# Second cross attention of a two-layer decoder: two steps of the query quantization move from VectorE to GpSimd

## What is computed

```python
def _fq_sym(x, axis):
    s = jnp.max(jnp.abs(x), axis=axis, keepdims=True) / 127.0
    s = jnp.maximum(s, 1e-08)
    q = jnp.clip(jnp.round(x / s), -127.0, 127.0) * s
    return x + jax.lax.stop_gradient(q - x)
...
q = (x @ Wq + bq).reshape(1, B * N, H, hd)      # 2048 rows, 16 heads of 16
kv = (cond @ Wkv + bkv).reshape(1, -1, 2, H, hd)  # 512 keys for all rows
...
attn = jax.nn.softmax(attn.astype(jnp.float32), axis=-1)
attn = _fq_unsigned(attn, axis=-1)
```

## Time and profile before

| | |
|---|---|
| median of 3 runs | 1367.86 us (1361.7 to 1369.36) |
| profiled execution: its own time | 1366.42 us |
| profiled execution: span | 1364.3 us |
| mean granted TensorE clock | 0.916 of full |
| second cross attention, first limit to last exponential | 781.4 to 1109 us |
| busy: TensorE / VectorE / ScalarE / GpSimd | 84% / 66% / 46% / 42% of the span |

### The profile page before, as it was taken

How to read it: one execution, slowest core, us unless ns; L and a number is a source line. 1 busy time by engine, 2 the same in 40 slices (tenths; PEclk the granted TensorE clock), 3 DMA queues, 4 the chain that set the end, 5 groups by cost and what they waited for, 6 DMA issues and landing times.

```text
span 1364.3 us, 24773 instructions
## 1 busy us (share of the span) xinstructions
PE 1140.4 (84%) x7640; PEld 809.8 (59%) x7679; DVE 898.8 (66%) x2501; ACT 632.9 (46%) x1432; POOL 577.2 (42%) x886
## 2 busy tenths in 40 slices
PE   3699989994999999668887677877777778999988
PEld 2577767772566666446665345655555554788755
DVE  5576764774432333388877399999999864656657
ACT  3165654331211111225554498988889851433300
POOL 6143542248211111125565354466655653455500
PEclk8799999995999999879898789888889778999989
DMA  5866735013111111265441300000000014455454
GB/s 146 199 202 157 198 106 175 27 48 110 52 47 47 47 42 44 79 176 152 120 127 33 125 4 1 6 29 33 29 18 29 25 40 136 128 161 157 146 180 144
DMA packets 75805, 127.10 MB, mean 93 GB/s; under 512 B 11703, under 2 KB 59063, under 8 KB 72279
## 3 DMA queue, kind: packets, MB, share of 16 engines
q1 hardware_dynamic: 62142, 95.13, 25.3%
q0 software_dynamic: 10272, 28.39, 5.7%
q10 hardware_dynamic: 3264, 2.01, 0.5%
HBM read 76.97 MB, written 48.13 MB: 92 GB/s over the span
## 4 chain that ended last, share of the span: by engine, by line
PE 56%; issue 12%; ACT 9%; POOL 9%; DVE 6%; DMA 5%; SPq 2%; ACTq 1%; POOLq 0%; DVEq 0%
PE ps L228 17%; PE ps L1173 15%; PE ps L1190 7%; ACT work L1917 6%; POOL work L1951 3%; PE ps L482 3%; POOL xs_scratch L1511 2%; PE ps L1182 2%; PE ps L1158 2%; DMA W<-work 2%; PE ps L495 1%; PE ps L464 1%; DVE work L608 1%; DMA W<-q_parts 1%; PE ps L508 1%
## 5 line engine op out<-in xcount | busy, mean ns | idle before, releaser
L1173 PE MATMUL ps<-W,work 128*128 x628 | 227.5, 495 | 1.6 <-issue 1.4
L1917 ACT ACTIVATE work<-ps,work 128x512 f32<-128x512 f32 x256 | 205.1, 821 | 40.4 <-POOL work L1951 39.1
L1529 POOL DMA_INDIRECT ys_scratch<-work x118 | 113.1, 958 | 260.2 <-DVE work L1373 113.4
L1855 DVE TENSOR_REDUCE work<-ps 128x1 f32<-128x512 f32 x256 | 172.7, 681 | 14.3 <-PE ps L1762 8.1
L1423 DVE TENSOR_TENSOR work<-work,ps 128x128 f32<-128x128 f32 (+1 forms) x118 | 49.7, 421 | 199.2 <-ACT work L1492 198.6
L608 DVE TENSOR_REDUCE work<-ps 128x2 f32<-128x512 f32 (+1 forms) x192 | 127.2, 685 | 71.4 <-PE ps L464 70.2
L787 POOL TENSOR_SCALAR_AFFINE_SELECT work<-work 128x256 f32<-128x256 f32 (+1 forms) x192 | 92.6, 485 | 157.5 <-ACT work L721 156.4
L1951 POOL TENSOR_SCALAR work<-work 128x1 f32<-128x1 f32 x256 | 99.8, 390 | 128.3 <-DVE work L1855 113.0
L1173 PEld LDWEIGHTS ps<-W,work 128*128 128x128 f32 x628 | 110.9, 191 | 68.9 <-issue 63.1
L721 ACT ACTIVATE work<-ps 128x512 f32<-128x512 f32 x192 | 110.6, 599 | 66.6 <-PE ps L482 66.0
L1492 ACT ACTIVATE work<-ps 128x128 f32<-128x128 f32 (+1 forms) x118 | 45.3, 384 | 164.7 <-PE ps L1173 164.7
(11 more groups left out here) (261 smaller groups left out, 2398.9 us busy)
## 6 DMA issues: line engine op xcount, KB each, us to landing
work<-xs_scratch SPq DMA_DIRECT2D x79, 132.0 KB, 2.2
W<-ys_scratch SPq DMA_DIRECT2D x16, 512.0 KB, 3.8
q_parts<-work SPq DMA_DIRECT2D x48, 128.0 KB, 1.9
W<-in_w_in SPq DMA_DIRECT2D x6, 1024.0 KB, 11.2
W<-q_parts SPq DMA_DIRECT2D x15, 384.0 KB
work<-xs_scratch SPq DMA_DIRECT2D x39, 130.0 KB, 2.1
W<-k_parts SPq DMA_DIRECT2D x8, 512.0 KB
W<-in_w_out SPq DMA_DIRECT2D x1, 4096.0 KB, 18.9
```

The costliest lines, as they stand in the source:

```text
L1173: mm = q.e.matmul(PS[bks[c]][:, 0:N], self.XT[s % 2][:, k, :], w[:, k, bass.ds(regs[s] + 512 * c if c else regs[s], N)], start=k == 0, sto ...
L1529: q.e.indirect_dma_start(YS[L], bass.IndirectOffsetOnAxis(ap=self.dst[n % self.NY], axis=0), self.YB[n % self.NY], None).then_inc(*landing ...
L1855: q.e.tensor_reduce(self.mm[:, h:h + 1], PS[banks.of["c1_s", t, h]][:, :], AX, ALU.max, negate=True).then_inc(*up("c1_mx", t, h))
L1917: q.e.activation(self.ee[n // 2 % 3][:, 512 * (h % 2):512 * (h % 2) + 512], PS[banks.of["c1_s", t, h]][:, :], ACT.Exp, bias=self.nb[:, h:h ...
```

## The change

VectorE's `dve_queries` ends with the reciprocal, which now raises the event "c1_rq". The multiplication and the rounding are issued by GpSimd in a new function `pool_queries`: the multiplication in round 8, ahead of a scatter where there is one, the rounding in round 9, and the clamp in round 10 as before, now behind GpSimd's own chain instead of VectorE's event. For tile 0 both are issued ahead of the first clamp. Operands, types and values are the same.

```diff
                 q.wait_ge(at("c1_sq", t))
-                e.reciprocal(self.rq, sq).then_inc(*q.step())
-                yield
-                q.wait_ge(q.chain())
-                e.tensor_tensor(q3, q3, bc(self.rq, 2, 16), ALU.mult).then_inc(*q.step())
-                yield
-                q.wait_ge(q.chain())
-                e.tensor_scalar(qf, qf, MAGIC, MAGIC, ALU.add, ALU.subtract).then_inc(*up("c1_qr", t))
+                e.reciprocal(self.rq, sq).then_inc(*up("c1_rq", t))
...
+            def pool_queries(self, q, t):
+
+                q3 = heads(self.qf, 16)
+                q.wait_ge(at("c1_rq", t))
+                q.e.tensor_tensor(q3, q3, bc(self.rq, 2, 16), ALU.mult).then_inc(*q.step())
+                yield
+                q.wait_ge(q.chain())
+                q.e.tensor_scalar(self.qf, self.qf, MAGIC, MAGIC, ALU.add, ALU.subtract).then_inc(*q.step())
+
             def pool_Q3(self, q, t):
-                q.wait_ge(at("c1_qr", t), at("c1_z"), at("c1_qt", t - 1))
+                q.wait_ge(q.chain(), at("c1_z"), at("c1_qt", t - 1))
...
                 pool_numbers(q, 1)
+                queries = [self.pool_queries(q, 0)]
+                steps(queries, 9)
                 self.pool_Q3(q, 0)
...
+                    if h == 8 and t + 1 < T:
+                        queries = [self.pool_queries(q, t + 1)]
+                    steps(queries)
                     if h == 10 and t + 1 < T:
                         self.pool_Q3(q, t + 1)
```

## The result

The changed kernel takes 1384.62 us (median of 4 runs, 1382.65 to 1389.89) against 1368.61 us of the kernel before (median of 4 runs, 1361.7 to 1375.82). The ratio is 1.0122, with a 95% interval of 1.0063 to 1.0182. Timed once more beside other kernels it was 1.0089 (1.0058 to 1.0119), so the loss is 12 to 17 us. The forecast was 1371, 3 us above before, and the range ended at 1383.

A forecast was written before the change was run, and what follows sets the result against it. VectorE has almost no idle time, but GpSimd, in order inside the head loop, is crowded in rounds 8 to 12. Terms 2.0 + 0.6 + 1.2 - 0.5 + 1.1 = +4.4 us on 1366.4 gave 1371, range 1362 to 1383.

The forecast's parts named there:

- That is where the two instructions are put: GpSimd, inside the head loop, crowded in rounds 8 to 12; TensorE waited 1.91 us for Q3, ScalarE 2.12 for a limit.
- The likeliest case: The forecast of 1371 us together with its neighbour, the start alone at about 1368; chance 0.60, own range 1365 to 1375.
- the second rival: GpSimd's burst in rounds 8 to 10 becomes the bound in full: +10 to +19 us, 1377 to 1386; chance 0.27.
- start: Tile 0, where nothing else runs: GpSimd's two instructions delay Q3 and all rounds by 1.1 us (bounds 1.0 and 1.3).
- tiles 0 to 2: Less LayerNorm and routing around; limit 7 to Q3 needs 3.2 us against 2.45: +0.4 us each, 1.2 in all.
- tile 3: No scatter, and limit 9 waited 1.32 us for VectorE: the cover holds, the whole 0.53 us is won, -0.5.
- even tiles from 4 on: GpSimd needs 3.2 us from limit 7 to Q3 instead of 2.75, limit 7 comes 0.34 earlier: +0.1 each, 0.6.
- odd tiles from 5 on: Five tiles with scatters: Q3 starts 0.16 us later, plus the port, +0.4 each (between +0.16 and +0.76), 2.0 in all.
- the reckoning from limit 7 to Q3: GpSimd's queue of limits, multiplication, rounding and what lies between, ahead of Q3: 3.2 us in even tiles, Q3 +0.16 in odd.
- the next is due two rounds later: VectorE's L1860 is done before GpSimd's rounding, so no term for a blocked L1860; otherwise 15 x 0.55 = 8 us.
- a Q3 held up by L1860: Odd tiles: L1860 comes 0.53 us earlier, ahead of Q3, which may stand behind it for up to 0.6 us.
- VectorE's 8 us turn into idle time: The 8.0 us of room freed on VectorE become idle time ahead of work that GpSimd releases later.

The follow-up runs named there:

- again: The changed kernel, profiled and timed a second time against the kernel before: ratio 1.0089, stage stretch +14.1 us.
- the version with the cheap operation: The changed kernel with GpSimd's rounding replaced by a clamp of the same operands, queries not rounded: 1.0027 of the kernel before, stage +3.4 us.
- the relief: From the changed kernel, GpSimd's multiplication and rounding taken out too, so neither engine does them: 0.9916 of the kernel before, stage -6.1 us.
- both sides: The changed kernel with VectorE also keeping both instructions, into a scratch tile: 1.0135 of the kernel before, stage +19.0 us.
- two rounds earlier: The changed kernel with its three GpSimd instructions in rounds 6, 7 and 8 instead of 8, 9 and 10: 1.0039 of the kernel before, stage +5.3 us.
- the run meant to part them: The changed kernel with TensorE's transposes of Q3 moved from round 12 to 14, ScalarE's copy from 13 to 15: 1.0308 of before, stage +43.2 us.
- the better kernel: The kernel before with only the multiplication on GpSimd and no scatter in rounds 8 and 10: 1362.88 us against 1371.85, ratio 0.9945.
- the one with the moved scatters: The changed kernel with the scatters of rounds 8 and 10 moved to later even rounds: 1.0027 of the kernel before, 1.0031 when run again.

## Why the prediction was wrong

- **Bound and place.** "That is where the two instructions are put" held, and so did VectorE's freed room becoming partly idle time. The likeliest case was forecast at 0.60 and the second rival, GpSimd's burst as the bound, at 0.27 with 1377 to 1386 us. The result is that rival's: (13.1 - 1.1) / 15 = 0.8 us a tile, where it had 0.6 to 1.23.
- **Prices of the instructions.** 0.62 and 1.14 us were forecast, 0.620 and 1.084 measured. The start was +1.1, and it is: from the first L1836 to the first Q3 2.19 us before, 3.32 after.
- **The terms of the sum**, against the growth of the stretches in the two profiles of the change (us; tile 14 ends behind the stage stretch):

| term | forecast | the change | again |
|---|---|---|---|
| start | +1.1 | +1.1 | +1.1 |
| tiles 0 to 2 | +1.2 | +1.1 | +2.7 |
| tile 3 | -0.5 | -0.4 | -0.4 |
| even tiles from 4 on | +0.6 | +4.1 | +3.9 |
| odd tiles from 5 on | +2.0 | +7.2 | +6.9 |

- **The step that failed** is the reckoning from limit 7 to Q3 in the even and odd tiles. Even tiles: 3.2 us forecast, 3.78 measured. Odd tiles: 4.44 forecast (4.28 + 0.16, before the allowance of about 0.25 for ports), 5.35 measured. In both most of the missing time is in instructions that got longer because they now overlap a VectorE rounding: limit 9 by 0.5 us, the power by 0.46, a scatter by 0.28. The text had the rule and the rows for it, and then gave it no term because "the next is due two rounds later". That is true of the GpSimd rounding, which met no VectorE rounding in tiles 6 and 7, and false of limit 9 and the power behind it. The term that it did have, a Q3 held up by L1860, isn't what happened: Q3 takes 0.83 us as before. That tiles 0 to 2 came out right in the first profile is luck: their three stretches grew by 1.08, -1.15 and 1.20.
- **Not seen at all:** the slow pairs in the rounds after the burst, where I had let the loss end at Q3. Of the 1.61 us that odd tile 7 grew by, 1.09 stand at Q3; it was 0.6 us shorter than before once the scatters were moved away and no slow pair was left. The growth of the odd tiles goes with the slow pairs in most of the table (13 slow pairs and 1.6 us a tile with the change, 1 and 0.1 us with the rounding alone), but that they are all of it isn't shown: the version with the cheap operation has 13 too, and its odd stretches grew by only 0.65 us.
- **"VectorE's 8 us turn into idle time"** was wrong in the other direction. Alone the relief is worth 6.1 us of stage and 0.84% of the time, and against "both sides" the change still gets 5.9 us of stage for it. By the forecast's own terms the GpSimd work was priced at 4.4 + 8.0 = 12.4 us; it costs 19.0, that is (19.0 - 1.1) / 15 = 1.19 us a tile of the 1.70 it lasts.
- **The Trainium skill's rule** on one-input work (GPSIMD Engine Reference, Engine selection) is again contradicted for this operation: 1084 ns on GpSimd for what took VectorE 287. The rule on the shared ports (SBUF — State Buffer, Practical consequences) is what the long limits show: 0.78 us for a limit that met a VectorE rounding, 0.26 for one that didn't. Which of the two took the ports first, the records don't show: the blocked limit's record starts 0.06 us earlier.
- **Open:** by which path the loss reaches the end of the tile. TensorE's wait for Q3 and ScalarE's wait for limits both grew by 13 us. With the first all but gone ("two rounds earlier") 5.3 us of loss are left, so it isn't the only one; the run meant to part them was confounded.

## What to carry to other kernels

An engine that is half idle on average can still stand in everybody's loop; then what counts is how much work lies between two of its short, awaited instructions, and an instruction moved there can cost most of its own length (here 0.7 of it, from one profile of each kernel) and not just what sticks out of the idle time. When a delay pushes a short instruction back, look up which long instruction of the engine that shares its ports comes next, and charge that collision too. Measure both halves of a move, the relief and the new load, by themselves: here one is worth -0.8%, the other +1.4%. Then measure each instruction of the move alone: the better kernel moves only the multiplication, which is neutral by itself, and leaves the rounding on VectorE. And compare by kind of tile before saying that parts add, since errors can cancel in a total.

## What was unexpected on the hardware

- Within GpSimd, 128x256 fp32 with two immediates takes 1084 ns for add and subtract, 400 ns for minimum and maximum, in the same place of the same kernel.
- The same rounds can run in two rhythms. With the same instructions in the same order, a scatter and two limits repeated every 2.11 to 2.13 us in the kernel before and in the one with the moved scatters, and every 2.46 us in the changed one, at full granted clock. What differs is what lay some rounds ahead of them; how that sets the rhythm isn't shown.
- Whether a short GpSimd instruction (128x1) takes 0.26 or 0.8 us turned on whether it started more or less than about 0.08 us ahead of VectorE's 128x1024 rounding.
